# A warm-up on TensorE, loads and matmuls in another order, and the idle row added and stored in sixteen pieces instead of eight

## The chip, the cores and the metric

One core of a Trainium2 chip runs the whole kernel in one launch. The metric is the device time of one execution in microseconds (us), as a median over runs. The core has TensorE (matrix products), VectorE, ScalarE, GpSimd and SyncE (SP, which issues DMAs), each with its own in-order queue; they wait for each other by semaphores only. Sixteen DMA engines move the data.

## The reference, cut to what matters

```python
# x: (2, 2048, 512), cond_1024: (2, 512), w1: (512, 2048), w2: (2048, 512), all float32
c = cond[:, None, :] + cumsum(relu(x) * 0.001, axis=1)     # over the 2048 tokens of a batch
spikes = (floor(c) - floor(previous c)) / 0.001             # 0 nearly everywhere
out = x + relu(spikes @ w1 + b1) @ w2 + b2
```

Every channel climbs slowly, so it crosses an integer at one token or at none. Most tokens have no spike at all: their added row is always the same, relu(b1) @ w2 + b2, the **idle row**. A token with one spike gets a row that depends on the channel alone, and all 512 such rows can be made ahead as a **table**. The few tokens with more than one spike, the **general** rows, need the real product.

## The kernel before

Each partition holds a block of 16 consecutive tokens, for each of the 2 batches (`x_sb0`, `x_sb1`, 32 KB a partition each). x comes in 16 pieces of two tokens a partition (512 KB, `load_x`), w1 turned and w2 in 16 pairs of 512 KB (`load_pair`), alternating on SP's queue; chunk 0 is loaded as two halves of 256 KB, and w2's half (`w2_first_in`, line 376) is issued by ScalarE with b1, cond (`start_c`) and b2 (lines 375 to 378). w1 as such (4 x 1 MB, line 276) follows on SP.

ScalarE turns each chunk of weights into relu(1000*w1 + b1) - relu(b1) (lines 383 and 384). TensorE multiplies it with w2 in 4 units a chunk, each of 512 columns and, in float32, of two passes (`table_part`, line 725). There are 16 chunks of 4 units; into them, in an order written by hand (lines 805 to 841), TensorE takes everything else: `add_strips` (line 738, relu(b1) @ w2 in four strips), `join_strips` (746), `turn_totals` (756, the totals of a batch turned to channel-major), `spread_tokens` (766), `count_leads` (772 to 777), `find_slots` (786). After the table come the real product's first layer (795, 16 groups) and second layer (802, 32 passes).

VectorE adds relu(x) over the 16 tokens of each block (`block_totals`, lines 476 and 478, one token an instruction), runs prefix sums over the blocks (`block_sums`), finds in which block each channel crosses (`find_blocks`), and, from sixteen values that GpSimd gathers (line 319), at which token (`find_tokens`). Then it counts which tokens are shared (`count_met`, `find_leads`), gives the general tokens slots (`find_slots`), and writes the general tokens' spikes (`first_spikes`, `second_spikes`). `finish_idle_row` and `add_idle` (line 614) add the idle row to x in place, in pieces of four tokens a partition, 4 a batch. SP stores each piece when it is added (`store_idle`, lines 278 to 284).

GpSimd waits until a batch is stored (`idle_stored`), then issues four indirect DMAs that add the table's rows to the single tokens' rows in DRAM (`add_row`, line 324), for each batch. At last it adds the general rows (line 339). `new_row` (line 650) is the product less its idle part. The loop for odd inputs (`redo`) doesn't run on these.

Of the kernel before, what the change touches and what calls it, by code (L numbers as in the profile page):

```python
# [6 lines left out]
ALU = mybir.AluOpType  # L7
# [6 lines left out]
P = 128  # L14
# [4 lines left out]
def spike_ffn(nc, x, x_turned, cond, cond_cols, w1, w_pairs, b1_cols, b2, out):  # L19
# [14 lines left out]
    XQ = 4  # L34
    TQ = BLK // XQ
# [4 lines left out]
    STRIPS = P // STRIP  # L40
    FAR = 4.0 * ROWS
# [8 lines left out]

    def piece(q):
        return slice(q * TQ, (q + 1) * TQ)

    with ExitStack() as ctx:
# [11 lines left out]
        w1_sb = sb("w1_sb", [P, DC, F])  # L66
        total = [sb(f"total{b}", [P, D]) for b in range(B)]
# [60 lines left out]
        none_far = sb("none_far", [P, 1])  # L128
        to_general = sb("to_general", [P, 1], I32)
# [52 lines left out]
        const_ready = sem("const_ready")  # L182
        pool_step = sem("pool_step")
# [21 lines left out]
        general_listed = sem("general_listed")  # L205
        odd_ready = sem("odd_ready")
# [7 lines left out]
        idle_added = [[sem(f"idle_added{b}_{q}") for q in range(XQ)] for b in range(B)]  # L214
# [39 lines left out]
        def _(sp):  # L254
# [26 lines left out]

            for b in range(B):
                for q in range(XQ):
                    store_idle(b, q)
            for b in range(B):
                sp.wait_ge(idle_stored[b], 16 * XQ)

        @block.gpsimd
        def _(pool):
# [33 lines left out]
            def add_row(to, row, done):  # L323
                pool.indirect_dma_start(out=out_rows, out_offset=bass.IndirectOffsetOnAxis(ap=to, axis=0),  # L324
                                        in_=row, in_offset=None, bounds_check=last_row, oob_is_err=False,
                                        compute_op=ALU.add).then_inc(done, 16)

            pool.wait_ge(singles_listed, 1)
            for b in range(B):
                pool.wait_ge(idle_stored[b], 16 * XQ)  # L330
                for c in range(DC):
                    col = b * DC + c
                    pool.wait_ge(table_rows_ready, c + 1)
                    add_row(to_single[:, col:col + 1], table_row[c], singles_scattered)
# [32 lines left out]
        def _(act):  # L367
# [60 lines left out]
        def _(dve):  # L428
# [42 lines left out]
            def block_totals(b, q):  # L471
                for t in range(q * TQ, (q + 1) * TQ):
                    if t % TH == 0:
                        dve.wait_ge(x_in[b][t // TH], 16)
                    if t == 0:
                        chain(dve.tensor_scalar(total[b][:, :], x_sb[b][:, 0, :], 0.0, None, ALU.max))
                    else:
                        last = dve.scalar_tensor_tensor(out=total[b][:, :], in0=x_sb[b][:, t, :], scalar=0.0,  # L478
                                                        in1=total[b][:, :], op0=ALU.max, op1=ALU.add)
                        if t < BLK - 1:  # L480
                            chain(last)
                        else:
                            last.then_inc(totals_ready, 1)
# [109 lines left out]
            def list_general():  # L593
                for b in range(B):
# [3 lines left out]
                chain(dve.tensor_scalar(none_far[:, :], slot_row[:, :], 0.5, FAR, ALU.is_lt, ALU.mult))  # L598
                dve.scalar_tensor_tensor(out=to_general[:, :], in0=slot_row[:, :], scalar=-1.0, in1=none_far[:, :],
                                         op0=ALU.add, op1=ALU.add).then_inc(general_listed, 1)  # L600
                chain(dve.tensor_scalar(crowd[:, :], check_sums[:, 0:1], P + 0.5, None, ALU.is_gt))
# [16 lines left out]
            for q in range(XQ):  # L618
                block_totals(0, q)
            block_totals(1, 0)  # L620
            block_sums(0)
            find_blocks(0)
            for q in range(1, XQ):
                block_totals(1, q)
# [16 lines left out]
            add_idle(0, 0)  # L641
            second_spikes()
            for q in range(1, XQ):
                add_idle(0, q)
            list_singles()
            for q in range(XQ):
                add_idle(1, q)
            list_general()
            dve.wait_ge(out_summed, 1)
# [253 lines left out]
```

## Time and profile before

| what | value |
|---|---|
| median of 3 runs | 113.02 us (112.84 to 113.58) |
| profiled execution | 113.63 us, its span 111.9 us |
| TensorE busy | 96.5 us (86%) |
| VectorE busy | 72.1 us (64%) |
| ScalarE busy | 35.1 us (31%) |
| GpSimd busy | 27.8 us (25%) |
| DMA | 31.40 MB, mean 281 GB/s |

The span is what the trace covers; the execution's time is 1.7 us longer. All times in the rows count from the span's start. PE is TensorE, PEld its weight loads, DVE VectorE, ACT ScalarE, POOL GpSimd; a name with q is the engine's sequencer, which issues DMAs or waits. A merged row says how many instructions it holds (x8).

### The profile page before, as it was taken

The page shows a single profiled execution, that of the slowest core. Times are in us where ns is not written, and L with a number is a line of the kernel's source. Part 1 is how long each engine was busy: PE and PEld are TensorE (multiplying, and loading weights), DVE is VectorE, ACT ScalarE, POOL GpSimd, SP SyncE. Part 2 cuts the span into 40 slices and gives each one's busy share as a digit, 9 for nine tenths or more (in the row PEclk, how much of TensorE's full clock was granted, in tenths as well). Part 3 has the DMA queues.
Part 4 walks back from the last instruction along what each step waited for, and adds up shares of the span by engine and source line. Part 5 has one row for each costly group of instructions (what it writes and reads, how often), then busy time and mean ns, then how long its engine had stood idle before and what let it go on. Part 6 is the DMA issues. An engine that isn't in the chain of part 4 may idle for free.

```text
span 111.9 us, 1155 instructions
## 1 busy us (share of the span) xinstructions
PE 96.5 (86%) x370; PEld 51.8 (46%) x370; DVE 72.1 (64%) x161; ACT 35.1 (31%) x65; POOL 27.8 (25%) x32
## 2 busy tenths in 40 slices
PE   0089999999999999999999999999999999996000
PEld 0043444444544244444344565669999844442000
DVE  2008976965689999788977578999999930002000
ACT  0997154145325249970200200007743300000000
POOL 6600000000005720007500000000004885087810
PEclk9999999999999999999999999999999999999965
DMA  3999999999999999999930000098999999957960
GB/s 93 345 329 316 419 420 412 410 410 410 409 413 404 411 390 395 392 387 386 378 101 0 0 0 0 6 366 337 419 419 419 413 297 373 187 70 96 105 79 8
DMA packets 10010, 31.40 MB, mean 281 GB/s; under 512 B 1682, under 2 KB 1810, under 8 KB 8976
## 3 DMA queue, kind: packets, MB, share of 16 engines
q1 hardware_dynamic: 7872, 29.10, 66.9%
q0 software_dynamic: 1552, 1.64, 10.5%
q10 hardware_dynamic: 576, 0.54, 1.7%
q8 instruction: 5, 0.08, 0.3%
q14 instruction: 5, 0.04, 0.1%
HBM read 21.31 MB, written 10.75 MB: 287 GB/s over the span
## 4 chain that ended last, share of the span: by engine, by line
PE 56%; POOL 10%; DVE 10%; issue 10%; DMA 4%; ACT 3%; ACTq 2%; POOLq 1%; DVEq 0%
PE ps_table L725 48%; POOL out L324 10%; DVE x_sb L614 8%; DMA out<-x_sb 4%; PE ps_idle L738 3%; PE ps_turn L756 2%; ACT L387 1%; DVE spk_t L574 1%; PE ps_met L786 1%; PE ps_idle L746 1%; ACT w_sb L384 1%; ACT w_sb L383 1%; DVE hot L557 1%; POOLq L249 0%; ACTq L376 0%
## 5 line engine op out<-in xcount | busy, mean ns | idle before, releaser
L725 PE MATMUL ps_table<-w_sb 128*128 128x512 f32 x128 | 59.9, 619 | 6.1 <-ACT w_sb L384 6.1
L725 PEld LDWEIGHTS ps_table<-w_sb 128*128 128x128 f32 x128 | 24.5, 198 | 36.1 <-issue 28.1
L478 DVE SCALAR_TENSOR_TENSOR total<-x_sb,total 128x512 f32<-128x512 f32 x30 | 20.8, 692 | 4.8 <-DMA x_sb<-in_x 3.9
L324 POOL DMA_INDIRECT out<-w_sb,to_single x8 | 14.2, 1772 | 35.7 <-DMA out<-x_sb 33.9
L383 ACT ACTIVATE w_sb<-w_sb,b_col 128x512 f32<-128x512 f32 (+2 forms) x20 | 12.6, 628 | 20.2 <-DMA w_sb<-in_w_pairs 20.2
L319 POOL DMA_INDIRECT rates<-in_x_turned,sixteen_at x8 | 8.4, 1047 | 41.9 <-DVE sixteen_at L504 40.0
L614 DVE TENSOR_TENSOR x_sb<-x_sb,idle_row 128x2048 f32<-128x2048 f32 x8 | 17.9, 2285 | 0.0
L802 PE MATMUL ps_idle<-w_sb 128*128 128x512 f32 x32 | 13.9, 592 | 0.0
L384 ACT ACTIVATE w_sb<-w_sb,minus_relu_b 128x512 f32<-128x512 f32 (+2 forms) x20 | 12.7, 636 | 0.7
L802 PEld LDWEIGHTS ps_idle<-w_sb 128*128 128x128 f32 x32 | 6.0, 190 | 7.2 <-issue 7.2
L795 PE MATMUL ps_small<-spk_t,w_sb 128*128 128x128 f32 x64 | 8.5, 275 | 0.0
L795 PE MATMUL ps_turn<-spk_t,w_sb 128*128 128x128 f32 x64 | 8.5, 275 | 0.0
L650 DVE TENSOR_TENSOR w_sb<-ps_idle,idle_base 128x512 f32<-128x512 f32 x1 | 0.7, 692 | 11.8 <-PE ps_idle L802 11.8
L795 PEld LDWEIGHTS ps_turn<-spk_t,w_sb 128*128 128x128 f32 x64 | 7.9, 192 | 0.5 <-issue 0.5
L795 PEld LDWEIGHTS ps_small<-spk_t,w_sb 128*128 128x128 f32 x64 | 7.8, 192 | 0.0
L404 ACT ACTIVATE w_sb<-ps_turn,b_col 128x128 f32<-128x128 f32 x8 | 2.9, 367 | 14.0 <-PE ps_turn L795 14.0
L452 DVE COPY start_t<-start_c 128x16 f32<-128x16 f32 x1 | 0.2, 174 | 6.1 <-DMA start_c<-in_cond_cols 6.1
L738 PE MATMUL ps_idle<-w_sb,relu_b 128*32 128x512 f32 x32 | 4.1, 601 | 0.0
L404 ACT ACTIVATE w_sb<-ps_small,b_col 128x128 f32<-128x128 f32 x8 | 2.9, 368 | 3.2 <-PE ps_small L795 3.2
L538 DVE SCALAR_TENSOR_TENSOR same<-ps_turn,token,weigh 128x512 bf16<-128x512 f32 x4 | 3.0, 751 | 1.4 <-PE ps_turn L766 1.3
L487 DVE TENSOR_TENSOR_SCAN level<-block_keep,ps_turn 128x512 f32<-128x512 bf16 x2 | 2.4, 1221 | 1.6 <-PE ps_turn L756 1.6
L538 DVE SCALAR_TENSOR_TENSOR same<-ps_met,token,weigh 128x512 bf16<-128x512 f32 x4 | 3.0, 751 | 0.1
(111 smaller groups left out, 52.7 us busy)
## 6 DMA issues: line engine op xcount, KB each, us to landing
x_sb<-in_x SPq DMA_DIRECT2D x16, 512.0 KB, 15.2
out<-x_sb SPq DMA_DIRECT2D x8, 1024.0 KB, 4.8
w_sb<-in_w_pairs SPq DMA_DIRECT2D x15, 512.0 KB, 16.2
w_sb<-in_w SPq DMA_DIRECT2D x4, 1024.0 KB, 17.2
w_sb<-in_w_pairs SPq DMA_DIRECT2D x1, 256.0 KB, 2.6
w_sb<-in_w_pairs ACTq DMA_DIRECT2D x1, 256.0 KB, 4.8
b_row<-in_b ACTq DMA_DIRECT2D x1, 256.0 KB, 8.6
rates<-in_x_turned,sixteen_at POOLq DMA_INDIRECT x8, 5.5
```

The lines of the kernel that those rows point to most:

```text
L319: pool.indirect_dma_start(out=rates[:, col, :], out_offset=None, in_=x_sixteen, in_offset=bass.IndirectOffsetOnAxis(ap=sixteen_at[:, col:c ...
L324: pool.indirect_dma_start(out=out_rows, out_offset=bass.IndirectOffsetOnAxis(ap=to, axis=0), in_=row, in_offset=None, bounds_check=last_ro ...
L383: chain(act.activation(weights, weights, ACT.Relu, bias=b1_col[:, m:m + 1], scale=PER_DT))
L384: act.activation(weights, weights, ACT.Identity, bias=minus_relu_b1[:, m:m + 1]).then_inc(table_hidden_ready, 1)
L404: act.activation(hidden[m], ps_hidden[m % 2][:, 0:P], ACT.Relu, bias=b1_col[:, m:m + 1], scale=PER_DT).then_inc(ready, 1)
L478: last = dve.scalar_tensor_tensor(out=total[b][:, :], in0=x_sb[b][:, t, :], scalar=0.0, in1=total[b][:, :], op0=ALU.max, op1=ALU.add)
L538: chain(dve.scalar_tensor_tensor(out=same[:, :], in0=ps_spread[b][:, :], scalar=token[:, col:col + 1], in1=weigh[:, (3 - c) * P:(7 - c) * ...
L614: dve.tensor_tensor(tokens, tokens, along(idle_row[:, :], TQ), ALU.add).then_inc(idle_added[b][q], 1)
L725: last = pe.matmul(ps_table[c][:, :], table_hidden[:, m, c * P:(c + 1) * P], w2_sb[:, m, :], start=(m == 0), stop=(m == FC - 1))
L738: last = pe.matmul(ps_idle[strip, :], relu_b1[:, m:m + 1].to_broadcast([P, STRIP]), w2_sb[:, m, :], start=(m < STRIPS), stop=(m >= FC - ST ...
L795: last = pe.matmul(ps_hidden[m % 2][:, 0:P], w1_sb[:, c, m * P:(m + 1) * P], spk_t[:, c, :], start=(c == 0), stop=(c == DC - 1))
L802: last = pe.matmul(ps_out[:, :], hidden[m], w2_sb[:, m, :], start=(m == 0), stop=(m == FC - 1))
```

## The change

Five things change:

- SP takes over three of ScalarE's DMAs: w2's first half goes second in its queue, cond after pair 1, b2 behind all pairs and ahead of w1. b1 stays with ScalarE.
- GpSimd fills `ones` first and tells TensorE, which multiplies ones by ones 8 times into a bank that is overwritten later, before the table.
- `block_totals` adds two tokens an instruction (1024 elements) into `total_two`, and joins the halves at the end.
- TensorE's order by hand: strips in other places, a unit of the table before or behind a small step.
- The idle row is added and stored in 16 pieces of two tokens (8 a batch). Two of them come before `second_spikes`. The general rows are no longer added to the stored ones: GpSimd gathers the x rows of the general tokens (`general_x`) between the two batches' scatters, VectorE adds b2 to them and then the product, and the last scatter writes plainly.

```diff
+    WARM = 8
...
             sp.dma_start(w_sb[:, 0, 0, :], w_pairs[0:P, 0, :]).then_inc(w_in[0], 16)
+            sp.dma_start(w_sb[:, 0, 1, :], w_pairs[0:P, 1, :]).then_inc(w2_first_in, 16)
             load_pair(1)
+            sp.dma_start(start_c[:, :], cond_cols).then_inc(start_in, 16)
             load_x(0)
...
+            sp.dma_start(b2_row[:, :], b2.rearrange("(o d) -> o d", o=1).to_broadcast([P, D])).then_inc(b2_in, 16)
             for i in range(WQ):
...
-            def store_idle(b, q):
-                sp.wait_ge(idle_added[b][q], 1)
-                sp.dma_start(out_blk[b, :, piece(q), :], x_sb[b][:, piece(q), :]).then_inc(idle_stored[b], 16)
+            def store_idle(b, h):
+                sp.wait_ge(idle_added[b], h + 1)
+                tokens = slice(h * TH, (h + 1) * TH)
+                sp.dma_start(out_blk[b, :, tokens, :], x_sb[b][:, tokens, :]).then_inc(idle_stored[b], 16)
...
+            chain(pool.memset(ones[:, :], 1.0))
+            pool.sem_inc(ones_ready, 1)
             chain(pool.memset(ident[:, :], 0.0))
             chain(pool.memset(ident_dt[:, :], 0.0))
-            chain(pool.memset(ones[:, :], 1.0))
...
             for b in range(B):
-                pool.wait_ge(idle_stored[b], 16 * XQ)
+                if b == 1:
+                    pool.wait_ge(general_listed, 1)
+                    pool.indirect_dma_start(out=general_x[:, :], out_offset=None, in_=x_rows,
+                                            in_offset=bass.IndirectOffsetOnAxis(ap=from_general[:, :], axis=0)
+                                            ).then_inc(general_got, 16)
+                pool.wait_ge(idle_stored[b], 16 * XH)
...
             redo = redo_count(pool)
-            pool.wait_ge(general_listed, 1)
             pool.wait_ge(row_ready, 1)
-            add_row(to_general[:, :], new_row, general_scattered)
+            pool.indirect_dma_start(out=out_rows, out_offset=bass.IndirectOffsetOnAxis(ap=to_general[:, :], axis=0),
+                                    in_=new_row, in_offset=None, bounds_check=last_row, oob_is_err=False
+                                    ).then_inc(general_scattered, 16)
...
             act.dma_start(b1_col[:, :], b1_cols).then_inc(b1_in, 16)
-            act.dma_start(w_sb[:, 0, 1, :], w_pairs[0:P, 1, :]).then_inc(w2_first_in, 16)
-            act.dma_start(start_c[:, :], cond_cols).then_inc(start_in, 16)
-            act.dma_start(b2_row[:, :], b2.rearrange("(o d) -> o d", o=1).to_broadcast([P, D])).then_inc(b2_in, 16)
...
+                for h in range(begin, end):
+                    dve.wait_ge(x_in[b][h], 16)
+                    tokens = x_sb[b][:, h * TH:(h + 1) * TH, :]
+                    if h == 0:
+                        chain(dve.tensor_scalar(total_two[b][:, :, :], tokens, 0.0, None, ALU.max))
                     else:
...
+                        chain(dve.scalar_tensor_tensor(out=total_two[b][:, :, :], in0=tokens, scalar=0.0,
+                                                       in1=total_two[b][:, :, :], op0=ALU.max, op1=ALU.add))
+                if end == XH:
+                    dve.tensor_tensor(total[b][:, :], total_two[b][:, 0, :], total_two[b][:, 1, :], ALU.add).then_inc(
+                        totals_ready, 1)
...
+                dve.tensor_scalar(from_general[:, :], slot_row[:, :], -1.0, 0.0, ALU.add, ALU.max)
...
-            def add_idle(b, q):
+            def add_idle(b, begin, end):
                 dve.wait_ge(idle_ready, 1)
-                tokens = x_sb[b][:, piece(q), :]
-                dve.tensor_tensor(tokens, tokens, along(idle_row[:, :], TQ), ALU.add).then_inc(idle_added[b][q], 1)
+                for h in range(begin, end):
+                    tokens = x_sb[b][:, h * TH:(h + 1) * TH, :]
+                    dve.tensor_tensor(tokens, tokens, along(idle_row[:, :], TH), ALU.add).then_inc(idle_added[b], 1)
...
-            add_idle(0, 0)
+            add_idle(0, 0, 2)
             second_spikes()
-            for q in range(1, XQ):
-                add_idle(0, q)
+            add_idle(0, 2, XH)
             list_singles()
-            for q in range(XQ):
-                add_idle(1, q)
+            add_idle(1, 0, XH)
             list_general()
+            judge()
+            dve.wait_ge(general_got, 16)
+            chain(dve.tensor_tensor(general_x[:, :], general_x[:, :], b2_row[:, :], ALU.add))
             dve.wait_ge(out_summed, 1)
-            dve.tensor_tensor(new_row, ps_out[:, :], idle_base[:, :], ALU.subtract).then_inc(row_ready, 1)
+            dve.tensor_tensor(new_row, ps_out[:, :], general_x[:, :], ALU.add).then_inc(row_ready, 1)
...
+            pe.wait_ge(ones_ready, 1)
+            for _ in range(WARM):
+                pe.matmul(ps_small[:, 0:P], ones[:, :], ones[:, :], start=True, stop=True)
             for c in range(DC):
                 table_part(0, c, c + 1)
             table_part(1, 0, 2)
             table_part(1, 2, DC)
-            for m in range(2, 5):
+            for m in range(2, 4):
                 table_chunk(m)
+            add_strips(0, 4)
+            table_chunk(4)
             table_part(5, 0, 3)
             turn_totals(0)
             table_part(5, 3, DC)
             table_chunk(6)
             table_chunk(7)
-            add_strips(0, 4)
+            add_strips(4, 8)
             table_chunk(8)
-            table_part(9, 0, 3)
+            table_part(9, 0, 2)
             turn_totals(1)
-            table_part(9, 3, DC)
-            add_strips(4, 8)
+            table_part(9, 2, DC)
             table_chunk(10)
-            table_part(11, 0, 2)
+            table_part(11, 0, 3)
             spread_tokens(0)
             add_strips(8, FC)
-            table_part(11, 2, DC)
-            table_part(12, 0, 3)
+            table_part(11, 3, DC)
+            table_part(12, 0, 1)
+            join_strips()
+            table_part(12, 1, 3)
             count_leads(0)
             table_part(12, 3, DC)
-            table_part(13, 0, 2)
+            table_part(13, 0, 1)
             spread_tokens(1)
-            join_strips()
-            table_part(13, 2, 3)
+            table_part(13, 1, 2)
             find_slots(0)
-            table_part(13, 3, DC)
+            table_part(13, 2, DC)
             table_part(14, 0, 2)
             count_leads(1)
             table_part(14, 2, DC)
-            table_part(15, 0, 1)
             find_slots(1)
-            table_part(15, 1, DC)
+            table_chunk(15)
```

## Rows read from the trace of the kernel before

**Rows 1.** Chain of waits: start us, us, what
```profile
37.37 0.99 PE ps_idle L738 x8
...
44.58 0.89 PE ps_turn L756 x8
...
68.21 0.24 PE ps_small L777 x2
...
69.85 2.29 DVE x_sb L614
...
97.49 0.50 POOLq L249
...
105.15 1.55 POOL out L324
```

**Rows 2.** Timeline of ScalarE (ACTq: its DMA issues): start us, us, engine, line, operation
```profile
0.80 0.40 ACTq L375 DMA_DIRECT2D b_col<-in_b_cols  x1
1.23 0.46 ACTq L376 DMA_DIRECT2D w_sb<-in_w_pairs  x1
...
2.69 1.28 ACT L387 ACT_TABLE_LOAD   x1 [2.69 <-issue]
...
4.91 0.40 ACT L384 ACTIVATE w_sb<-w_sb,minus_relu_b 128x128 f32<-128x128 f32 x1
...
39.22 0.72 ACT L384 ACTIVATE w_sb<-w_sb,minus_relu_b 128x512 f32<-128x512 f32 x1
```

**Rows 3.** DMA issues of the whole span: queue, count, KB each, us to landing
```profile
w_sb<-in_w_pairs ACTq DMA_DIRECT2D x1, 256.0 KB, 4.8
...
b_col<-in_b_cols ACTq DMA_DIRECT2D x1, 8.0 KB, 2.8
...
out<-w_sb,to_general POOLq DMA_INDIRECT x1, 4.8
```

**Rows 4.** Timeline of TensorE's weight loads: each begins one pass of 512 columns
```profile
10.54 0.34 PEld L725 LDWEIGHTS ps_table<-w_sb 128*128 128x128 f32 x1 [0.52 <-issue]
11.40 0.22 PEld L725 LDWEIGHTS ps_table<-w_sb 128*128 128x128 f32 x1 [0.52 <-issue]
11.86 0.19 PEld L725 LDWEIGHTS ps_table<-w_sb 128*128 128x128 f32 x1 [0.24 <-issue]
```

**Rows 5.** Timeline of TensorE's matmuls, last group
```profile
88.71 13.90 PE L802 MATMUL ps_idle<-w_sb 128*128 128x512 f32 x32
```

**Rows 6.** DMA issues of 0 to 1.3 us, and of 22.05 to 22.2 us
```profile
w_sb<-in_w_pairs SPq DMA_DIRECT2D x1, 512.0 KB, 4.5
...
x_sb<-in_x SPq DMA_DIRECT2D x1, 512.0 KB, 17.7
```

**Rows 7.** Timeline of SP, its last x piece
```profile
22.07 2.98 SPq L261 DMA_DIRECT2D x_sb<-in_x  x1
```

**Rows 8.** Timeline of VectorE
```profile
34.06 8.67 DVE L478 SCALAR_TENSOR_TENSOR total<-x_sb,total 128x512 f32<-128x512 f32 x12
...
73.10 6.68 DVE L614 TENSOR_TENSOR x_sb<-x_sb,idle_row 128x2048 f32<-128x2048 f32 x3
...
90.03 0.16 DVE L599 SCALAR_TENSOR_TENSOR to_general<-slot_row,none_far 128x1 int32<-128x1 f32 x1
```

**Rows 9.** Four stretches: us, TensorE busy, PEclk, DMA share, GB/s
```profile
13.00:34.00 21.00, 21.00 (x56) 1.00 1.03 412
76.20:84.00 7.80, 7.80 (x72) 1.00 1.02 420
84.00:97.00 13.00, 13.00 (x64) 1.00 1.02 349
...
72.00:73.00 1.00, 1.00 (x4) 1.00 0.00 0
```

**Rows 10.** Timeline of GpSimd
```profile
53.99 0.95 POOL L319 DMA_INDIRECT rates<-in_x_turned,sixteen_at  x1 [0.31 <-issue]
...
92.69 1.55 POOL L324 DMA_INDIRECT out<-w_sb,to_single  x1 [0.30 <-issue]
```

More of the change, by code:

```diff
@@ L66, in spike_ffn @@
         w1_sb = sb("w1_sb", [P, DC, F])
+        total_two = [sb(f"total_two{b}", [P, TH, D]) for b in range(B)]
         total = [sb(f"total{b}", [P, D]) for b in range(B)]
@@ L128, in spike_ffn @@
         none_far = sb("none_far", [P, 1])
+        from_general = sb("from_general", [P, 1], I32)
+        general_x = sb("general_x", [P, D])
         to_general = sb("to_general", [P, 1], I32)
@@ L182, in spike_ffn @@
         const_ready = sem("const_ready")
+        ones_ready = sem("ones_ready")
         pool_step = sem("pool_step")
@@ L213, in spike_ffn @@
         idle_ready = sem("idle_ready")
-        idle_added = [[sem(f"idle_added{b}_{q}") for q in range(XQ)] for b in range(B)]
+        idle_added = [sem(f"idle_added{b}") for b in range(B)]
         idle_stored = [sem(f"idle_stored{b}") for b in range(B)]
@@ L276, in _ @@
                 sp.dma_start(w1_sb[:, :, part], w1.rearrange("(c p) f -> p c f", p=P)[:, :, part]).then_inc(w1_in[i], 16)
-            def store_idle(b, q):
-                sp.wait_ge(idle_added[b][q], 1)
-                sp.dma_start(out_blk[b, :, piece(q), :], x_sb[b][:, piece(q), :]).then_inc(idle_stored[b], 16)
+            def store_idle(b, h):
+                sp.wait_ge(idle_added[b], h + 1)
+                tokens = slice(h * TH, (h + 1) * TH)
+                sp.dma_start(out_blk[b, :, tokens, :], x_sb[b][:, tokens, :]).then_inc(idle_stored[b], 16)
             for b in range(B):
-                for q in range(XQ):
-                    store_idle(b, q)
+                for h in range(XH):
+                    store_idle(b, h)
             for b in range(B):
-                sp.wait_ge(idle_stored[b], 16 * XQ)
+                sp.wait_ge(idle_stored[b], 16 * XH)
         @block.gpsimd
@@ L321, in _, with add_row @@
                                             ).then_inc(sixteen_got[b], 16)
-            def add_row(to, row, done):
+            def add_row(to, row):
                 pool.indirect_dma_start(out=out_rows, out_offset=bass.IndirectOffsetOnAxis(ap=to, axis=0),
                                         in_=row, in_offset=None, bounds_check=last_row, oob_is_err=False,
-                                        compute_op=ALU.add).then_inc(done, 16)
+                                        compute_op=ALU.add).then_inc(singles_scattered, 16)
             pool.wait_ge(singles_listed, 1)
             for b in range(B):
-                pool.wait_ge(idle_stored[b], 16 * XQ)
+                if b == 1:
[4 more added lines that the diff above has]
+                pool.wait_ge(idle_stored[b], 16 * XH)
                 for c in range(DC):
@@ L469, in names, with block_totals @@
                 dve.tensor_scalar(strip_first[:, :], strip_i[:, :], 0.0, None, ALU.is_equal).then_inc(strip_first_ready, 1)
[L471 to L476, printed above, removed]
-                    else:
[L478 to L483, printed above, removed]
+            def block_totals(b, begin, end):
+                for h in range(begin, end):
[3 more added lines that the diff above has]
+                        chain(dve.tensor_scalar(total_two[b][:, :, :], tokens, 0.0, None, ALU.max))
+                    else:
+                        chain(dve.scalar_tensor_tensor(out=total_two[b][:, :, :], in0=tokens, scalar=0.0,
[3 more added lines that the diff above has]
+                        totals_ready, 1)
             def block_sums(b):
@@ L609, in finish_idle_row @@
                 dve.tensor_tensor(idle_row[:, :], b2_row[:, :], idle_base[:, :], ALU.add).then_inc(idle_ready, 1)
-            def add_idle(b, q):
+            def add_idle(b, begin, end):
                 dve.wait_ge(idle_ready, 1)
-                tokens = x_sb[b][:, piece(q), :]
-                dve.tensor_tensor(tokens, tokens, along(idle_row[:, :], TQ), ALU.add).then_inc(idle_added[b][q], 1)
+                for h in range(begin, end):
+                    tokens = x_sb[b][:, h * TH:(h + 1) * TH, :]
+                    dve.tensor_tensor(tokens, tokens, along(idle_row[:, :], TH), ALU.add).then_inc(idle_added[b], 1)
             rise_levels()
             names()
-            for q in range(XQ):
-                block_totals(0, q)
-            block_totals(1, 0)
+            block_totals(0, 0, XH)
+            block_totals(1, 0, 2)
             block_sums(0)
             find_blocks(0)
-            for q in range(1, XQ):
-                block_totals(1, q)
+            block_totals(1, 2, XH)
             find_bases(0)
```

12 lines of the change are left out of this document (4 added, 8 removed).

## Prediction

> **What bounds the kernel now.** I read the chain of waits first, then each engine's timeline around its links. The chain [rows 1] ends in the last DMA that GpSimd issues, the scatter of the general rows at 105.15. Before it GpSimd issues batch 1's four scatters of single rows, and those began only when batch 1's last store had landed (97.49). So this path decides the end: VectorE's idle adds, the stores, four scatters, one scatter. The adds start at 69.85, and what releases them is TensorE: it is never without work from 6.14 on (96.5 of busy time), and VectorE's slot step waits for the last of its lead counts, at 68.21. TensorE has an end of its own close behind: the last row's matmuls run from 88.71 to 102.61 [rows 5], so the row is ready at about 103.3, 1.8 before GpSimd can take it. A gain must therefore come on TensorE's schedule before 69.85, and it is worth only as much as both the stores and the last matmuls follow.
>
> **1. TensorE starts earlier.** ScalarE issues four DMAs, then loads its table until 3.97, and its first scaled weights are ready at 5.31 [rows 2]. TensorE still starts only at 6.14, since the other operand, w2's first half-pair, was issued at 1.23 and takes 4.8 [rows 2, 3]: 6.03. After, ScalarE issues one DMA, so the table load is over by about 2.5 and b1's landing decides: 0.80 + 2.8 = 3.6, with 0.1 of waking 3.7. From there the same steps take 5.31 - 3.97 = 1.34: 5.05. The w2 half goes second in SP's queue. A whole pair, issued at this place, landed after 4.5 [rows 6], about 5.75; half the bytes put it before 5. Start 5.1 instead of 6.14: **-1.05**.
>
> **2. The ones.** The weight loads show TensorE's pace: one pass of 512 columns each 0.86 until 11.40, and 0.46, soon 0.43, from then on [rows 4]. That is a factor of two, the 1.2 and the 2.4 GHz level. From the first pass to the change are 11.40 - 6.14 = 5.26, at half speed: 2.63 lost. GpSimd's memset of the ones now comes first, so the 8 matmuls (16 passes) can start near 1.3. Eight passes of 128 columns take 0.89 at the fast level [rows 1], so 16 at the slow one take 3.6 and end at 4.9, before the table may start: they cost nothing. If the rate again rises 5.26 after the first pass, it rises at 6.56, and the table loses (6.56 - 5.1)/2 = 0.73 instead of 2.63: **-1.9**. Bounds: nothing lost (another 0.7 better), and no help at all (1.9 worse).
> The Trainium skill (TensorE: Matmul & The Clock Gate, Part 1) says that activity releases the throttle and that the point moves from run to run, since the window in which the chip looks does not start with the kernel. By it 5.26 would be one draw, and my sum would move between those same bounds; the trace has one execution and can't show the spread.
>
> **3. Order on TensorE.** Strips 0 to 8 now come before the second turn of the totals, instead of 0 to 4 (+0.99), and one unit of chunk 9 comes after it instead of before (-0.86) [rows 1, 4]. The turn of 44.58 thus comes 2.95 - 0.13 = 2.8 earlier, at 41.8. Its input must be there: the last x piece is issued at 22.07 and takes 17.7 [rows 6, 7], 39.8; b2's 262 KB now go behind all pairs, which at 412 GB/s [rows 9] gives 0.64: 39.15. Then VectorE needs one two-token step and the joining add. Twelve one-token steps took 8.67, 0.72 each; 2048 elements take 2.2 [rows 8]; a 1024 step lies between, 1.2. So totals are ready at 39.15 + 1.2 + 0.7 = 41.05. That leaves 0.7 of slack; before, they were done at 42.7 with 1.8 of slack. Weights are not late either: chunk 9, scaled by 39.94 before [rows 2], is ready near 39.3, and TensorE comes for it at 41.8 less two units, 40.1. The moved strips are what keeps TensorE busy until there. Behind the turn the same work remains, with join, spread and slots shifted by a unit; VectorE's inputs to them shift alike. I take 0 for waits there.
>
> **4. The adds.** The last lead count and all behind it come 2.95 earlier; the adds start at 66.9. The second spikes follow after two half-pieces (2.4), and are over near 70.4, while TensorE wants them when the table is done, over a microsecond later.
>
> **5. The stores.** The first is issued after 1024 elements a partition, at 66.9 + 1.2 = 68.1, not at 69.85 + 2.29 = 72.14 [rows 1]: 4.0 earlier. From then on DMA is the slower one: 8.39 MB at 420 GB/s [rows 9] is 20, or 1.25 a piece, against adds of 1.2. 16 adds cost 19.2 instead of 17.6, and stay hidden under the stores. While batch 0's scatters run, DMA falls to 349 GB/s [rows 9]; these scatters also come 4.0 earlier and fall on the same part of the stores. Batch 1 would be stored 4.0 earlier, less the new gather of x rows, 262 KB: 0.64. So 97.49 becomes 94.1: **-3.4**. GpSimd has time for the gather's issue: its first four scatters end at 94.24 - 4.0 = 90.25 [rows 10]; the list, ready at 90.2 before [rows 8], comes 2.95 earlier and 1.6 later for the adds, 88.85; the issue takes 0.95 (the other gathers') to 1.55 (a scatter's) [rows 10] and is over by 92.1.
> Pieces of half the size are not seen among the stores. The nearest row is that of the loads, 512 KB each with 4 KB a partition: 412 GB/s, against 420 in the 1 MB stores [rows 9]. That is 2%, 0.4 over all stores; I leave it to the range.
>
> **6. The end.** Four scatters follow, one each 1.86 (1.55 and 0.30 between) [rows 10], so the last one's turn comes at 105.15 - 3.4 = 101.8. The row is ready at 102.61 - 2.95 + 0.7 = 100.4; the new add of general_x lies in VectorE's idle time before it. The last scatter now writes without adding. It takes 4.8 from issue to landing [rows 3]; if the adding was what made its issue longer than a gather's, 0.6 goes, if not, nothing. I take 0.3. The rest (start_c earlier, fewer steps on the totals, the split list and judge) lies beside DMA or TensorE and ends nothing.
>
> **Sum.** Profiled execution 113.63 (span 111.9): -3.4 - 0.3 = 109.9. It lay 0.6 above the median of the runs, 113.02; with that, 109.3, and with a tenth for small stores **109.4**.
>
> **Rivals.** A, *the ones don't lift the rate* (the change doesn't do what it says): then TensorE gains 1.05 alone and every later term is 1.9 worse: 111.3. For it: passes of 128 columns alone have not been seen to raise the rate here. Against: it does not fall through the first layer, 16 groups of such passes, after which the wide ones run at 13.90/32 = 0.43 [rows 5]. 0.12.
> B, *the small stores are slow*, the slower side. Place: SP's 16 stores. If each of the eight additional ones brings a dead time instead of overlapping with its neighbour, the end moves by eight times that. DMA moves nothing in the microsecond in which the first store is issued (72.14 to 73 at least, 0.8) [rows 9]; eight such are 6.4, and the time 115.8. It decides from 3.6/8 = 0.45 of dead time each. Against: the queued loads ran without gaps for 21 us (DMA share 1.03, same rows). 0.05 for slower, and 0.04 for half of it, which ends within 1%.
> The Trainium skill (DMA: Bandwidth & Descriptors, Bandwidth) advises batches of 1 MiB or more for 75% of peak. By an estimate from that page's peak of 436 GB/s the stores would need over 25.7 instead of 20, and the kernel would come out some 2 slower. The 412 GB/s of the queued 512 KB loads speak against it here.
> C, *the stores come out better and the last row decides*: with b2 out of the first loads these can gain more than 0.64, the gather may cost less, and TensorE may be fast from the start. Then GpSimd is free before the row: issue at 100.4 - 0.7 = 99.7, with the old tail of 6.75 a span of 106.4, a time of 108.2, less 0.3 for the plain write and 0.6 for the median 107.3. 0.14.
> D, *late data stops TensorE* at the second turn, which has lost a microsecond of slack: 0.5 to 2 more, 109.9 to 111.4. 0.05.
>
> **Numbers.** My forecast 0.60, A 0.12, B 0.09, C 0.14, D 0.05. The range goes from C's end to A's, 107.3 to 111.5. This kernel's runs can tell about 1% from no change: faster than 111.9 are all but B and a bad mixture of A and D, 0.89; within 1% 0.06; slower 0.05.
>
> **What would show it.** After: the table starts near 5.1 and its passes turn to 0.43 near 6.6; the second turn comes near 41.8 with no idle time before it; adds start near 66.9, the first store is issued near 68.1, and DMA moves 410 GB/s or more through sixteen; batch 1's last store lands near 94.1; the general scatter is issued near 101.8. I am wrong if passes stay at 0.86 until 8 or later, if DMA has holes between stores, or if GpSimd waits for the row rather than for its own scatters.

## The result and the profile after

The changed kernel takes 109.7 us (median of 4 runs, 109.19 to 110.0), the one before 113.3 in the runs beside it (112.84 to 115.35): a ratio of 0.969, 95% interval 0.963 to 0.976. A second comparison on another occasion gave 109.29 and a ratio of 0.962 (0.956 to 0.967). The forecast was 109.4. A few executions take over 1.5% more than the fastest of their kernel (here the 115.35; without it the median before is 113.02); the ratios leave them out, and where that moves the median of an experiment by more than 0.1, so does the time given.

The chain of waits of the changed kernel (start us, us, what) has the same links as [rows 1]:

```profile
35.55 0.99 PE ps_idle L750 x8
36.55 5.35 PE ps_table L737 x12
41.90 0.89 PE ps_turn L768 x8
...
65.20 0.24 PE ps_small L789 x2
...
66.84 2.36 DVE x_sb L627 x2
...
94.65 0.50 POOLq L250
...
102.33 1.04 POOL out L349
```

The reader is to see that the turn of the totals comes at 41.90 instead of 44.58, that no wait stands before it, and that the lead counts and the adds follow 3.01 earlier each (65.20 for 68.21, 66.84 for 69.85). GpSimd's wait for batch 1's stores ends at 94.65 instead of 97.49, only 2.84 earlier. The last scatter is issued at 102.33 instead of 105.15, and the span ends at 107.8 instead of 111.9: after the issue 5.46 are left instead of 6.75.

The timeline of ScalarE, to be held against [rows 2]:

```profile
0.80 0.39 ACTq L387 DMA_DIRECT2D b_col<-in_b_cols  x1
1.23 1.28 ACT L396 ACT_TABLE_LOAD   x1 [1.23 <-PEq L896]
3.75 0.21 ACT L396 ACTIVATE relu_b<-b_col 128x16 f32<-128x16 f32 x1 [1.24 <-DMA b_col<-in_b_cols]
...
4.68 0.40 ACT L393 ACTIVATE w_sb<-w_sb,minus_relu_b 128x128 f32<-128x128 f32 x1
```

The table load is over at 2.51, b1's landing decides, and the first scaled weights are ready at 5.08. TensorE's weight loads, against [rows 4], first the ones and then the table:

```profile
1.11 3.49 PEld L819 LDWEIGHTS ps_small<-ones 128*128 128x128 f32 x16 [1.11 <-POOLq L303]
5.13 0.50 PEld L737 LDWEIGHTS ps_table<-w_sb 128*128 128x128 f32 x2 [0.54 <-ACT w_sb L393]
6.14 0.31 PEld L737 LDWEIGHTS ps_table<-w_sb 128*128 128x128 f32 x1 [0.52 <-ACT w_sb L393]
6.70 0.19 PEld L737 LDWEIGHTS ps_table<-w_sb 128*128 128x128 f32 x1 [0.24 <-issue]
7.13 0.19 PEld L737 LDWEIGHTS ps_table<-w_sb 128*128 128x128 f32 x1 [0.24 <-issue]
```

The distance between loads shrinks to 0.56 behind 6.14 and is 0.43 from 6.70: the rate rose near 6.45, where it rose at 11.40 before. The last row's matmuls (against [rows 5]), then the two adds of VectorE at the end:

```profile
85.70 13.90 PE L814 MATMUL ps_idle<-w_sb 128*128 128x512 f32 x32
```

```profile
96.92 0.69 DVE L660 TENSOR_TENSOR general_x<-general_x,b_row 128x512 f32<-128x512 f32 x1 [8.43 <-DMA general_x<-in_x,from_general]
99.71 0.69 DVE L662 TENSOR_TENSOR w_sb<-ps_idle,general_x 128x512 f32<-128x512 f32 x1 [2.10 <-PE ps_idle L814]
```

The row is ready at 100.40. GpSimd takes it at 102.33, so as before its own queue decides, and not TensorE. GpSimd's timeline, against [rows 10]:

```profile
82.25 2.46 POOL L330 DMA_INDIRECT out<-w_sb,to_single  x1 [30.01 <-DMA out<-x_sb]
...
89.07 1.55 POOL L330 DMA_INDIRECT out<-w_sb,to_single  x1 [0.30 <-issue]
90.93 1.02 POOL L338 DMA_INDIRECT general_x<-in_x,from_general  x1 [0.30 <-issue]
94.88 1.57 POOL L330 DMA_INDIRECT out<-w_sb,to_single  x1 [2.93 <-DMA out<-x_sb]
```

The gather of x rows ends at 91.95 and GpSimd then waits 2.93 for the stores: the gather takes none of the time that counts on this queue. Three stretches of the changed kernel (us, TensorE's busy time, PEclk, DMA share, GB/s), against [rows 9]:

```profile
13.00:34.00 21.00, 21.00 (x61) 1.00 1.03 411
75.00:81.00 6.00, 6.00 (x56) 1.00 1.02 403
84.00:94.00 10.00, 10.00 (x37) 1.00 1.05 317
```

The loads run at the same rate as before. The smaller stores run at 403 GB/s, with the engines as full as ever.

### The profile page after: what moved, and what is told of

Its sections match the earlier page's. It is cut to its first block, busy times and chain, and to the rows that moved or that the text cites. A ratio compares the mean times of both kernels' runs of the same rounds, so it can differ in the third digit from the quotient of the medians.

```text
span 107.8 us, 1193 instructions
## 1 busy us (share of the span) xinstructions
PE 98.2 (91%) x386; PEld 54.6 (51%) x386; DVE 71.7 (67%) x157; ACT 35.1 (33%) x65; POOL 29.0 (27%) x33
## 4 chain that ended last, share of the span: by engine, by line
PE 56%; POOL 13%; DVE 11%; issue 8%; DMA 7%; ACT 1%; POOLq 1%; DVEq 0%
PE ps_table L737 48%; POOL out L330 11%; DVE x_sb L627 9%; DMA out<-x_sb 4%; PE ps_idle L750 4%; DMA b_col<-in_b_cols 3%; PE ps_turn L768 2%; POOL out L349 1%; DVE spk_t L583 1%; POOL general_x L338 1%; PE ps_met L798 1%; PE ps_idle L758 1%; DVE hot L566 1%; POOLq L250 0%; PE ps_turn L778 0%
## 5 line engine op out<-in xcount | busy, mean ns | idle before, releaser
L737 PE MATMUL ps_table<-w_sb 128*128 128x512 f32 x128 | 58.1, 602 | 0.2 <-ACT w_sb L393 0.2
L737 PEld LDWEIGHTS ps_table<-w_sb 128*128 128x128 f32 x128 | 23.8, 193 | 28.7 <-issue 27.4
L330 POOL DMA_INDIRECT out<-w_sb,to_single x8 | 13.7, 1712 | 34.8 <-DMA out<-x_sb 32.9
L488 DVE SCALAR_TENSOR_TENSOR total_two<-x_sb,total_two 128x1024 f32<-128x1024 f32 x14 | 17.1, 1225 | 6.0 <-DMA x_sb<-in_x 5.7
L325 POOL DMA_INDIRECT rates<-in_x_turned,sixteen_at x8 | 9.6, 1196 | 37.9 <-DVE sixteen_at L513 36.1
L627 DVE TENSOR_TENSOR x_sb<-x_sb,idle_row 128x1024 f32<-128x1024 f32 x16 | 18.4, 1221 | 0.0
L660 DVE TENSOR_TENSOR general_x<-general_x,b_row 128x512 f32<-128x512 f32 x1 | 0.7, 691 | 8.4 <-DMA general_x<-in_x,from_general 8.4
L819 PE MATMUL ps_small<-ones 128*128 128x128 f32 x16 | 3.8, 431 | 1.1 <-POOLq L303 1.1
L819 PEld LDWEIGHTS ps_small<-ones 128*128 128x128 f32 x16 | 3.5, 330 | 1.1 <-POOLq L303 1.1
```

Of the source, the lines that this page charges most:

```text
L325: pool.indirect_dma_start(out=rates[:, col, :], out_offset=None, in_=x_sixteen, in_offset=bass.IndirectOffsetOnAxis(ap=sixteen_at[:, col:c ...
L488: chain(dve.scalar_tensor_tensor(out=total_two[b][:, :, :], in0=tokens, scalar=0.0, in1=total_two[b][:, :, :], op0=ALU.max, op1=ALU.add))
L627: dve.tensor_tensor(tokens, tokens, along(idle_row[:, :], TH), ALU.add).then_inc(idle_added[b], 1)
L737: last = pe.matmul(ps_table[c][:, :], table_hidden[:, m, c * P:(c + 1) * P], w2_sb[:, m, :], start=(m == 0), stop=(m == FC - 1))
L819: pe.matmul(ps_small[:, 0:P], ones[:, :], ones[:, :], start=True, stop=True)
```

## The experiments

Twelve runs were made, in three groups, each with the kernel before beside it. To compare them apart from TensorE's schedule, which moves from run to run (below), I use the interval from VectorE's first idle add to GpSimd's first scatter of batch 1. It is 97.72 - 69.85 = 27.87 in the kernel before and 94.88 - 66.84 = 28.04 in the changed one. Two executions whose stores and scatters are the same as the changed kernel's gave 95.25 - 67.21 = 28.04 (the repetition) and 96.19 - 68.66 = 27.53 (without the ones), so differences of half a microsecond can't be read from it.

**The changed kernel again.**

> The changed kernel once more, for the runs beside it. Expected 109.7, table's passes turning fast within 1 us of 6.5 if the point moves from run to run, else at 6.45 again.

109.29 (108.81 to 110.46), ratio 0.962. The two values of the changed kernel, 109.7 and 109.29, say how far two occasions lie apart. In the profiled execution the passes turned fast near 7.2, not near 6.45 again: the point moves from run to run, and the adds, at 67.21, moved with it.

**Without the ones.**

```diff
-            for _ in range(WARM):
-                pe.matmul(ps_small[:, 0:P], ones[:, :], ones[:, :], start=True, stop=True)
```

> The changed kernel without the 8 matmuls of ones. Theory (TensorE's schedule decides and the ones only bring the fast rate forward): passes stay at 0.86 for some 5.3 us from 5.1, the second turn of the totals and everything behind it come 1.9 to 2.0 later (43.9), time 111.6. Rival (the loads have become the floor, the rate hardly matters): turn near 42.3, time 110.1 or less.

111.53, ratio 0.983 (0.976 to 0.990), 2.2 more than the changed kernel beside it. TensorE's weight loads:

```profile
8.86 0.34 PEld L737 LDWEIGHTS ps_table<-w_sb 128*128 128x128 f32 x1 [0.52 <-issue]
9.71 0.29 PEld L737 LDWEIGHTS ps_table<-w_sb 128*128 128x128 f32 x1 [0.52 <-issue]
10.24 0.19 PEld L737 LDWEIGHTS ps_table<-w_sb 128*128 128x128 f32 x1 [0.24 <-issue]
10.67 0.19 PEld L737 LDWEIGHTS ps_table<-w_sb 128*128 128x128 f32 x1 [0.24 <-issue]
```

Passes stay at 0.85 until about 9.9, and the second turn comes at 43.73 (41.90 with the ones). The loads are no floor yet: the rival (turn near 42.3) is out.

**Stores of 1 MB again, adds in 16 pieces.** SP waits for two pieces and stores them together:

```diff
+                if h % 2 == 0:
+                    return
                 sp.wait_ge(idle_added[b], h + 1)
-                tokens = slice(h * TH, (h + 1) * TH)
+                tokens = slice((h - 1) * TH, (h + 1) * TH)
```

> Adds still in 16 pieces, stores again 8 of 1 MB. Theory 'the first issue counts': first store issued 1.15 later (69.25), batch 1 stored 1.15 later (95.7), time 110.8. Rival 'the pause for the second spikes swallows it': the larger first store keeps DMA busy over that pause, the larger pieces run at 420 instead of 403 GB/s, batch 1 stored at 94.2, time 109.4.

110.03, ratio 0.970 (0.964 to 0.976), 0.7 more than the changed kernel. Its rate over 75 to 81 us:

```profile
75.00:81.00 6.00, 6.00 (x56) 1.00 1.03 423
```

Its adds start at 66.19, batch 1's first scatter at 94.93, an interval of 28.74. By these traces sixteen stores are worth 0.70 against eight, of the 1.15 by which they start earlier, and the lower rate would take the rest back. Both theories may have a part of it; but 0.70 is little more than the 0.5 by which the interval differs with the same stores, and the two ratios' intervals overlap, so the size isn't shown.

**General rows added again.** No gather, the product less its idle part, the last scatter with `compute_op=ALU.add`:

```diff
-                                    in_=new_row, in_offset=None, bounds_check=last_row, oob_is_err=False
-                                    ).then_inc(general_scattered, 16)
+                                    in_=new_row, in_offset=None, bounds_check=last_row, oob_is_err=False,
+                                    compute_op=ALU.add).then_inc(general_scattered, 16)
```

> The changed kernel with the general rows added again (no gather of x rows, product less its idle part, the last scatter accumulates). Theory: batch 1 stored 0.6 earlier (94.0) without the gather, last scatter issued near 101.7, but 0.5 more of issue and 0.8 more to landing behind it: span 108.5, time 110.4. Rival (the short tail of the changed kernel has nothing to do with the plain write): time 109.1.

110.83, ratio 0.973 (0.967 to 0.980), 1.5 more. GpSimd's timeline there:

```profile
95.07 1.55 POOL L330 DMA_INDIRECT out<-w_sb,to_single  x1 [4.25 <-DMA out<-x_sb]
...
102.50 1.55 POOL L345 DMA_INDIRECT out<-w_sb,to_general  x1 [0.30 <-issue]
```

The interval is 95.07 - 67.03 = 28.04, that with the gather, so the gather costs the stores nothing that can be seen. Behind the last issue lie 109.12 - 102.50 = 6.62, against 5.46 with the plain write: 1.16, of which 0.51 is the issue.

**The old loads.** ScalarE issues w2's half, cond and b2 again, and SP no longer does.

```diff
             act.dma_start(b1_col[:, :], b1_cols).then_inc(b1_in, 16)
+            act.dma_start(w_sb[:, 0, 1, :], w_pairs[0:P, 1, :]).then_inc(w2_first_in, 16)
+            act.dma_start(start_c[:, :], cond_cols).then_inc(start_in, 16)
+            act.dma_start(b2_row[:, :], b2.rearrange("(o d) -> o d", o=1).to_broadcast([P, D])).then_inc(b2_in, 16)
```

> The changed kernel with w2's half, cond and b2 again issued by ScalarE. Theory: table starts 1.0 later (6.1), but the rate is up by then or nearly, so that only 0.4 to 0.8 of it comes through; loads behind b2 0.6 to 1.2 later, second turn near 42.3; time 110.0. Rival (the two gains simply add up, TensorE goes slow again over the longer gap between ones and table): turn 1.0 to 2.9 later, time 110.6 to 112.

110.46, ratio 0.978 (0.973 to 0.983), between what the two theories said. The table starts at 6.02, 1.42 behind the ones, and runs at 0.43 a pass from there. The ones' loads were slow to the last (3.49 for the sixteen, as in the changed kernel), so the rate rose behind them, and this gap did not keep it from doing so. The adds start at 67.44, 0.60 later. The rest of the difference is in GpSimd's first scatter, 5.86 instead of 2.46; see the gaps between the adds, below.

**The kernel before with the ones alone** (their memset first, 8 matmuls ahead of the table).

```diff
+            pe.wait_ge(ones_ready, 1)
+            for _ in range(8):
+                pe.matmul(ps_small[:, 0:P], ones[:, :], ones[:, :], start=True, stop=True)
             for c in range(DC):
                 table_part(0, c, c + 1)
```

> The kernel before with only the ones added (memset first, 8 matmuls). Theory: table still starts at 6.14, all or nearly all passes fast, second turn 2.0 to 2.6 earlier (42.0 to 42.6) if the totals are there (42.7 in the kernel before, so they are not: TensorE waits, turn near 42.9); the rest 1.7 earlier; time 113.5 - 1.7 = 111.8. Rival (the loads are late too): gain under 1, time over 112.5.

Ratio 0.991 (0.985 to 0.996), 1.0 faster, with an interval of 0.4 to 1.6: under the 1.7 expected, and not apart from the rival's 'under 1'. Its twelve executions spread widely, from 111.1 to 114.78, and the median of all of them is 112.65. In the profiled one (114.37) w2's half landed late, at 7.9, so its schedule can't be compared; it shows what a long gap does, first the weight loads, then the stretch of 8 to 10 us with the columns of [rows 9]:

```profile
1.11 3.24 PEld L809 LDWEIGHTS ps_small<-ones 128*128 128x128 f32 x16 [1.11 <-POOLq L299]
8.00 0.50 PEld L727 LDWEIGHTS ps_table<-w_sb 128*128 128x128 f32 x2 [3.65 <-ACT w_sb L386]
9.02 0.34 PEld L727 LDWEIGHTS ps_table<-w_sb 128*128 128x128 f32 x1 [0.52 <-ACT w_sb L386]
9.87 0.34 PEld L727 LDWEIGHTS ps_table<-w_sb 128*128 128x128 f32 x1 [0.52 <-issue]
```

```profile
8.00:10.00 2.00, 1.97 (x3) 0.50 0.99 312
```

With 3.65 without a load behind the ones, the first table passes take 0.85 again, to beyond 10.7, and the granted clock of that stretch is 0.50, the 1.2 GHz level; from 11 on it is 1.00. The rate had been up before: the ones' sixteen loads took 3.24, not 3.49. (In the other traces the clock column says 1.00 over the slow passes of the start too, so there the pace of the loads has to tell.) The ones help only if the table follows closely: behind a gap of 1.42 (the old loads) the table was fast, behind 3.65 it was slow. What keeps this kernel from the full 1.7 in the other runs isn't settled; the totals as a floor (ready at 42.7) remain an argument.

**TensorE's old order in the changed kernel** (the lines from the first chunks to chunk 15 as before).

```diff
-            for m in range(2, 4):
+            for m in range(2, 5):
                 table_chunk(m)
-            add_strips(0, 4)
-            table_chunk(4)
...
-            add_strips(4, 8)
+            add_strips(0, 4)
             table_chunk(8)
```

> The changed kernel with TensorE's order of before. Theory (the order matters by what it does at the second turn and with waits for weights): strips 0 to 4 no longer fill, chunk 8 and 9 find TensorE 1.0 earlier, waits for weights of under 1 in all; what is behind the second turn holds the strips 4 to 8 again. Lead counts come as before within 0.5; slots(1) one unit later; time 109.5 to 110.2. Rival (the order carries a large part of the gain): over 1 later, time above 110.7.

110.19, ratio 0.974 (0.971 to 0.978). The adds start at 66.90, as in the changed kernel (66.84), with a rate that rose 0.4 earlier, which is worth 0.2: the order is worth 0.3 at most. The time comes from GpSimd, whose first scatter of batch 0 is issued like this:

```profile
82.33 5.85 POOL L330 DMA_INDIRECT out<-w_sb,to_single  x1 [30.15 <-DMA out<-x_sb]
88.48 1.57 POOL L330 DMA_INDIRECT out<-w_sb,to_single  x1 [0.30 <-issue]
```

Here, and with the old loads, GpSimd comes out of its batch 0 work (four scatters and the gather) at 95.39 and 95.93, later than the stores allow: it has no wait left before batch 1.

**Gaps between the adds.** The kernel just told of, with one wait more:

```diff
                     dve.tensor_tensor(tokens, tokens, along(idle_row[:, :], TH), ALU.add).then_inc(idle_added[b], 1)
+                    if b == 1:
+                        dve.wait_ge(idle_added[b], h + 1)
```

> The changed kernel with TensorE's old order, in which GpSimd's first scatter took 5.85 and ended 1.5 after VectorE's last add; here VectorE waits for each of batch 1's adds to be done before the next. Theory (VectorE's unbroken adds keep GpSimd from writing its descriptors): first scatter back to 2.5 or less, GpSimd waits for the stores again, last scatter issued 0.5 to 0.9 earlier than 102.85, time 109.5. Rival (the 5.85 is something else, such as code loading): still near 5.85, time 110.2.

109.24, ratio 0.966 (0.961 to 0.970), 0.9 less than without the wait; the intervals of the two ratios do not touch.

```profile
81.27 2.55 POOL L330 DMA_INDIRECT out<-w_sb,to_single  x1 [29.47 <-DMA out<-x_sb]
84.12 2.15 POOL L330 DMA_INDIRECT out<-w_sb,to_single  x1 [0.30 <-issue]
```

The 5.85 ended at 88.18, exactly 1.50 behind VectorE's last add (86.68); in the old-loads kernel the 5.86 ended at 88.72, 1.50 behind it too (87.22). With a gap between the adds, which costs VectorE 0.11 each (10.04 for eight instead of 9.17), the wait is gone. So VectorE's unbroken adds kept the scatter's issue from going on; that much is shown. What isn't shown is when they do. The changed kernel's adds are as unbroken, and there the scatter took 2.46, though it began 4.80 behind batch 1's first add, and the one of 5.85 began 4.82 behind it. With the gaps the scatter also began a microsecond earlier (81.27), and that may have a part in the cure.

**The early add.** The idle row is made before the second batch's tokens, one half-piece is added before the first spikes, two before the second.

```diff
             find_odd()
+            finish_idle_row()
...
-            finish_idle_row()
+            add_idle(0, 0, 1)
             first_spikes()
             find_slots(1)
-            add_idle(0, 0, 2)
+            add_idle(0, 1, 3)
```

> A version that might be better. The idle row is made in VectorE's gap before the second batch's tokens, one half-piece is added before the first spikes (VectorE's slack against TensorE there is about 1.0), two more before the second spikes. Theory (stores are bound by DMA from their first issue on): first store issued near 65.2 instead of 68.1, but DMA then waits for the next ones; batch 1 stored 1.0 earlier (93.7), last scatter issued near 101.4, time 108.3. Rival (TensorE now waits for slots or spikes): slots(1) or the first layer later by 0.4 or more, no gain.

109.34, ratio 0.967 (0.962 to 0.972): no gain. The adds begin at 63.47, and TensorE loses only 0.14 at batch 1's slots. But from the lead counts to batch 1's first scatter it is 94.00 - 64.33 = 29.67, against 94.88 - 65.06 = 29.82: of the expected microsecond 0.15 is left, which is less than the interval can tell. Behind the early store DMA runs dry, since the next adds aren't there (columns of [rows 9]):

```profile
67.00:68.00 1.00, 1.00 (x7) 1.00 0.00 0
68.00:69.00 1.00, 1.00 (x3) 1.00 0.30 123
...
71.00:72.00 1.00, 1.00 (x11) 1.00 0.30 115
```

An earlier first store alone doesn't bring the last one forward.

**32 stores of 256 KB.**

```diff
-                tokens = slice(h * TH, (h + 1) * TH)
-                sp.dma_start(out_blk[b, :, tokens, :], x_sb[b][:, tokens, :]).then_inc(idle_stored[b], 16)
+                for t in range(h * TH, (h + 1) * TH):
+                    sp.dma_start(out_blk[b, :, t:t + 1, :], x_sb[b][:, t:t + 1, :]).then_inc(idle_stored[b], 16)
```

> The changed kernel with every half-piece stored by two DMAs of 256 KB, 32 in all. Rival B (a dead time with each store): 16 more of them at 0.45 to 0.85 each, batch 1 stored 7 us or more later, time above 116. Theory (stores overlap, only the rate falls a little with the packet: 420 at 8 KB, 403 at 4 KB): 2 KB packets at some 370 to 385, batch 1 stored 1 to 2 later, time 110.5 to 111.

113.18, ratio 1.000 (0.996 to 1.003): it gives back the whole gain, 3.5 to 3.9. The interval is 98.06 - 66.82 = 31.24, 3.2 more, 0.20 for each additional store. The stretch with stores alone:

```profile
75.00:81.00 6.00, 6.00 (x57) 1.00 1.02 380
```

The engines are busy throughout, so no idle time stands between the stores, and the rate falls as expected (423, 403, 380 for 8, 4 and 2 KB a partition). But the time expected from that, 110.5 to 111, is missed by over 2, and the rival's 116 too. By the rate alone 8.39 MB need 20.8 at 403 and 22.1 at 380, 1.3 more; the other 1.9 arise elsewhere, in part where stores and scatters overlap (297 GB/s over 84 to 94 us, for 317), and how is open.

**Batch 0's scatters held back** until batch 1 is stored.

```diff
+                if b == 0:
+                    pool.wait_ge(idle_stored[1], 16 * XH)
```

> The changed kernel with batch 0's scatters held until batch 1 is stored too. Theory (the scatters' traffic slows the stores by some 3 us): the stores land near 91.3, GpSimd's first scatter begins at 91.4, nine scatters and a gather in a row, the last issued near 107.7, time 114.9. Rival (they don't disturb the stores): stores land at 94.6 as before, the last scatter is issued at 111, time 118.

116.44, ratio 1.028 (1.024 to 1.032), midway between the 114.9 of the theory and the rival's 118. The first lines of GpSimd's timeline, and its last:

```profile
93.02 1.62 POOL L330 DMA_INDIRECT out<-w_sb,to_single  x1 [40.64 <-DMA out<-x_sb]
...
109.31 1.04 POOL L351 DMA_INDIRECT out<-w_sb,to_general  x1 [0.30 <-issue]
```

The interval is 93.02 - 66.65 = 26.37, 1.67 less: that, not 3.3, is what the scatters' traffic costs the stores. The direction was right, the size by half.

**A version that might have been better**: the early add, seven matmuls of ones, and VectorE making relu(b1) and its negative.

```diff
             act.wait_ge(b1_in, 16)
-            act.activation(relu_b1[:, :], b1_col[:, :], ACT.Relu).then_inc(b1_ready, 1)
...
+            dve.wait_ge(b1_in, 16)
+            dve.tensor_scalar(minus_relu_b1[:, :], b1_col[:, :], 0.0, -1.0, ALU.max, ALU.mult).then_inc(b1_ready, 1)
+            dve.tensor_scalar(relu_b1[:, :], b1_col[:, :], 0.0, None, ALU.max).then_inc(b1_ready, 1)
```

> A version that might be better: the early add of the version before, and relu(b1) and its negative made by VectorE instead of ScalarE, so that ScalarE's first scaling waits for b1 alone; 7 matmuls of ones. Theory: table starts near 4.65 instead of 5.1, which is worth 0.25 to 0.45 at the second turn; all later terms follow; time 108.9. Rival (the loads are the floor by now): no gain over 109.3.

109.98, ratio 0.972 (0.967 to 0.977): not better. ScalarE's timeline shows why:

```profile
3.58 1.28 ACT L392 ACT_TABLE_LOAD   x1 [3.58 <-DMA w_sb<-in_w_pairs]
4.88 0.40 ACT L392 ACTIVATE w_sb<-w_sb,b_col 128x128 f32<-128x128 f32 x1
```

The table load stands with the first activation, and here that one sits behind the wait for the weights. The load of 1.28, hidden under b1's DMA in the changed kernel, moved onto the path, and the table started at 5.76 instead of the expected 4.65 (5.13 in the changed kernel). An activation on other data ahead of the waits might hide it again; that was not tried. None of these versions beats the changed kernel.

## Why the prediction was right, and which of its terms were not

The time was right (109.4 for 109.7), and so was the main part of the mechanism: TensorE's schedule moves the adds, the stores and GpSimd's queue follow. Part of the closeness is luck. Two terms were wrong in opposite directions: the stores gave 0.56 less than forecast, the last scatter 0.99 more, so that the profiled execution came out 0.4 shorter than the sum said. Against that, I had taken 0.6 off because the profiled execution before lay above its median; this time it lay 0.17 below (109.53 and 109.7).

- **Steps 1 and 2, start and ones.** Forecast 5.1 and 6.56 for the start and the change of rate, -2.95 in sum. Measured 5.13, about 6.45 and -3.01 at the adds. Without the ones the second turn is 1.83 later (forecast 1.9). Rival A is out. The value of the ones is a draw, as the expectation from the clock said: the rate rose near 6.45 in this execution, 7.2 in the repetition, 6.9 with general rows added, 6.0 in the old order, and before the table's first pass in those with the early add, with eight stores and with the old loads. That it fell so near the forecast 6.56 is luck too; the adds start between 66.19 and 67.21 by it (with w2's loads as in the changed kernel).
- **Step 3, order.** The turn was forecast at 41.8 and came at 41.90. The totals were done at 40.48 (forecast 41.05), so it didn't wait. That the reordering itself brings nearly nothing was in the +0.13; the old order starts its adds within 0.1, or 0.3 when the earlier rate is allowed for.
- **Step 4.** Adds at 66.84 (66.9).
- **Step 5, the stores, the step that was mis-sized.** Forecast -3.4 for batch 1 stored, measured -2.84. The first store was issued 4.0 earlier, as said (68.09). I then let everything behind it follow by 4.0, less 0.64 for the gather. The runs show the gather at nothing (28.04 with and without it), and an early first store that hardly helps the last one (0.15 in the version with the early add). From the first store's issue to batch 1's first scatter the kernel before takes 97.72 - 72.17 = 25.55 and the changed one 94.88 - 68.09 = 26.79, 1.24 more. The lower rate of the smaller pieces, which I left to the range with 2%, explains 0.8 of it (8.39 MB at 403 against 420 GB/s, 4%); the last 0.4 is open and within what the interval varies by. By the sign that I had set, 410 GB/s or more through sixteen stores, this step failed: they ran at 403, and at 264 over 70.84 to 72.84, where the second spikes hold up the third add (the kernel before has such a dip too, 205 over 75 to 76). From the first add to batch 1's first scatter the changed kernel needs 28.04 where the one before needed 27.87: all of the -2.84 is TensorE's 3.01. So halving adds and stores together brought nothing; the halved stores save something, 0.70 by the traces, only against 16 adds with whole stores.
- **Step 6, the plain write.** Forecast -0.3, measured -1.29 between the traces (6.75 to 5.46 behind the issue), and 1.16 against the same kernel with the add. I had bounded it by the gather's shorter issue (0.6, measured 0.51) and forgotten that the adding itself could lengthen the landing: it takes 3.4 instead of 4.8 from issue to landing (4.7 in the kernel that adds again).
- **Rival B** had its place right and its mechanism wrong: once the adds are ahead, DMA shows no holes between small stores (share 1.02 with 32 of them), they only move less. With 16 of them the price is small; with 32 the whole gain is gone. The advice of the Trainium skill (DMA: Bandwidth & Descriptors, Bandwidth), 1 MiB or more, is borne out in direction and not in size: 512 KB still runs at 403 GB/s.
- **Rival D**: TensorE waited for no data at the second turn, which found its totals done 1.4 before.
- **Rival C** stayed 1.9 away: the row was ready at 100.40, as computed, and GpSimd took it at 102.33.
- **A cost that I had not seen**: the issue of the scatters depends on VectorE. In the changed kernel it happened to be mild (2.46 for the first); in two neighbours of it GpSimd became the bound, and the time was longer by 0.5 to 0.9 for it.

## What to carry to other kernels

A warm-up on TensorE pays where the engine is the schedule's bound and real work follows it without a long gap; its worth is half of the slow time that it covers. When a tail is a queue of GpSimd scatters, look at each one's price separately: a plain write instead of an accumulating one saved more here than all the splitting of stores. An earlier first transfer is not an earlier last one, if what it carries runs out before the next is ready.

## What the runs showed of the hardware that was not expected

- **VectorE can hold up GpSimd's indirect DMAs.** A scatter's issue takes 1.55 alone, 1.90 to 2.55 beside VectorE's adds of two tokens (up to 3.01 beside those of four in the kernel before), and 5.85 where it came through only behind the last add. The Trainium skill (SBUF — State Buffer, SBUF: two separate sides) tells of a port pair that VectorE and GpSimd share and that one of them holds for a whole instruction: VectorE in a fast mode, or with two SBUF inputs against a GpSimd operation that reads SBUF. It has GpSimd unable to write a DMA's descriptors meanwhile, but says so of the fast mode only. The adds here have two SBUF inputs; the wait of 5.85, ended 1.50 behind the last add and gone with a gap between adds, agrees with a port that is held. Which of the port's rules applies can't be told from these runs, nor why the changed kernel's own scatter, as far into the adds, was spared.
- **The rate of TensorE rises on passes of 128 columns too**: in the version with the early add the ones alone had raised it, the first five table passes took 2.41, 0.48 each; and it fell again over 3.65 without a weight load (granted clock 0.50); behind 1.42 without one the table was fast.
- **Stores to DRAM** ran at 423, 403 and 380 GB/s with 8, 4 and 2 KB a partition.
- **An indirect scatter that accumulates** costs 0.51 more to issue than a plain one (1.55 for 1.04), and 1.16 more until the end.
